# Second attention: 64 more columns of the square on VectorE, whose share moves behind the next slot's first maximum

## What is computed

```
S = einsum("bhnd,bhmd->bhnm", Q, K) / dh ** 0.5
W_tau = softmax(S, axis=-1)
W_sigma = 1.0 / ((1.0 + abs(S) / beta) ** 2 + t ** 2)
W_sigma = W_sigma / W_sigma.sum(axis=-1, keepdims=True)
tau = einsum("bhnm,bhmd->bhnd", W_tau, V)
sigma = einsum("bhnm,bhmd->bhnd", W_sigma, V)
f = 0.5 * tau + 0.5 * sigma
```

## Time and profile before

| | before |
|---|---|
| median of 3 runs | 2976.28 us (2976.19 to 2976.68) |
| profiled execution: its time | 2972.06 us |
| its span in the trace | 2970.4 us |
| busy over the span: PE, DVE, ACT, POOL | 82%, 84%, 75%, 67% |
| product L1761, 256 times | 940.7 us busy, 3675 ns each |
| shift L1758, 256 times | 506.7 us busy, 1979 ns each |
| maximum L1967, 512 times | 618.3 us busy, 1208 ns each |
| sign operation L1978, 512 times | 614.9 us busy, 1201 ns each |
| share of the square L1985, 256 times | 247.7 us busy, 968 ns each |

### The profile page before, as it was taken

The page is one execution under the profiler, slowest core; times in us unless marked ns, Lnnn a source line. Parts: engine busy times, 40 slices in busy tenths (PEclk is TensorE's granted clock), DMA queues, the critical chain, the costliest instruction groups (busy, mean ns, idle before and its releaser), DMA issues. The chain is left out here.

```text
span 2970.4 us, 60006 instructions
## 1 busy us (share of the span) xinstructions
PE 2445.4 (82%) x18487; PEld 1018.8 (34%) x18614; DVE 2491.1 (84%) x3983; ACT 2234.4 (75%) x2441; POOL 1992.1 (67%) x1236
## 2 busy tenths in 40 slices
PE   3755999998577994689999999999999999983898
PEld 2642333333474662122222222222222222222566
DVE  4666888885577657799999999999999999996765
ACT  4532777777364543499999999999999999993554
POOL 4510222222453651499999999999999999994465
PEclk9976999999687997699999999999999999997799
DMA  3222111000120002000000000000000000000000
GB/s 116 70 64 87 30 29 29 28 27 11 45 79 5 1 0 86 22 15 14 16 15 14 14 16 15 14 14 16 15 14 14 16 15 14 14 5 0 1 12 18
DMA packets 93504, 76.58 MB, mean 26 GB/s; under 512 B 32480, under 2 KB 73960, under 8 KB 93264
## 3 DMA queue, kind: packets, MB, share of 16 engines
q1 hardware_dynamic: 89104, 66.36, 7.8%
q0 software_dynamic: 4288, 8.82, 0.9%
HBM read 47.77 MB, written 24.42 MB: 24 GB/s over the span
## 5 line engine op out<-in xcount | busy, mean ns | idle before, releaser
L1761 POOL TENSOR_TENSOR a_sg<-a_sg,all_f0w 128x1632 f32<-128x1632 f32 x256 | 940.7, 3675 | 21.3
L1967 DVE TENSOR_REDUCE a_mx<-a_pm 128x1 f32<-128x1024 f32 x512 | 618.3, 1208 | 23.2 <-PE a_pm L1813 23.2
L1978 DVE TENSOR_SCALAR a_sg<-a_pa 128x1024 int32<-128x1024 int32 x512 | 614.9, 1201 | 3.8 <-PE a_pa L1813 3.8
L1894 ACT ACTIVATE a_pt<-a_pb 128x1024 f32<-128x1024 f32 x512 | 532.4, 1040 | 55.0 <-PE a_pb L1813 53.4
L1831 PE MATMUL a_po<-a_pt,a_Vh 128*32 128x512 f32 x2048 | 538.4, 604 | 15.0 <-ACT a_osb L1913 11.4
L1831 PE MATMUL a_po<-a_sg,a_Vh 128*32 128x512 f32 x2048 | 538.3, 604 | 0.0
L1758 POOL TENSOR_SCALAR all_f0w<-a_sg,a_parh 128x1632 f32<-128x1632 f32 x256 | 506.7, 1979 | 37.4 <-DVE a_sg L1978 37.3
L1903 ACT ACTIVATE a_sg<-a_sg,a_parh 128x2048 f32<-128x2048 f32 x256 | 517.0, 2020 | 0.0
L1907 ACT ACTIVATE a_sg<-a_sg 128x2048 f32<-128x2048 f32 x256 | 496.0, 1937 | 0.0
L1581 ACT ACTIVATE a_pt<-a_ring 128x1024 f32<-128x1024 f32 (+2 forms) x384 | 313.7, 846 | 164.4 <-PE a_ring L1508 161.2
L1653 DVE TENSOR_REDUCE a_mx<-a_ring 128x2 f32<-128x1024 f32 (+3 forms) x384 | 359.2, 955 | 85.1 <-PE a_ring L1491 66.1
(11 more groups left out here) (265 smaller groups left out, 4457.9 us busy)
## 6 DMA issues: line engine op xcount, KB each, us to landing
all_Q<-q_parts SPq DMA_DIRECT2D x256, 48.0 KB
all_K<-k_parts SPq DMA_DIRECT2D x256, 48.0 KB
k_parts<-p_parts SPq DMA_DIRECT2D x16, 384.0 KB, 2.6
e_recs<-routed_rows SPq DMA_DIRECT2D x70, 64.5 KB, 1.9
n_xn<-expert_rows SPq DMA_DIRECT2D x16, 256.0 KB, 4.2
all_Q<-a_rows SPq DMA_DIRECT2D x256, 2.0 KB
q_parts<-p_parts SPq DMA_DIRECT2D x16, 192.0 KB, 2.3
q_parts<-p_parts SPq DMA_DIRECT2D x8, 384.0 KB, 2.6
```

Of the source, the lines that this page charges most:

```text
L1761: nc.gpsimd.tensor_tensor(buf[:, :, 0:CUT], buf[:, :, 0:CUT], sums, ALU.mult)\
L1894: nc.scalar.activation(pt[(j - LT) % 4][:, i, :], pb[:], ACT.Exp, scale=SC)\
L1967: nc.vector.tensor_reduce(mx[:, (j // PER) % 2, t:t + 1], pm[:], AX.X, ALU.max)\
L1978: nc.vector.tensor_scalar(sg[(j - LS) % 4][:, i, :].bitcast(I32), pa[:].bitcast(I32), SIGN_OFF, None, ALU.bitwise_and).then_inc(abs_done, 1)
```

## The change

Two edits in `attend_both`. `CUT` goes from 51 to 49 sixty-fourths of T, from 816 to 784 columns. GpSimd's two instructions shrink from 1632 to 1568 elements, and VectorE's share grows from 416 to 480. And that share is no longer issued at the end of its slot, but a slot later, behind the first maximum and ahead of everything else of that slot; what it waits for is named by the lag LS + 1.

```diff
-    CUT = 51 * T // 64
+    CUT = 49 * T // 64
...
                             nc.vector.tensor_reduce(mx[:, (j // PER) % 2, t:t + 1], pm[:], AX.X, ALU.max)\
                                 .then_inc(max_red, 1)
+                        sq = at(it, j, LS + 1)
+                        if i == 0 and sq is not None:
+                            buf = sg[(j - LS - 1) % 4]
+                            dve.wait_ge(abs_done, 2 * sq + 2)
+                            if (j - LS - 1) % PER == 0:
+                                dve.wait_ge(head_in[ring(j, LS + 1)], HEAD_LOADS * rounds(it, j, LS + 1))
+                            nc.vector.scalar_tensor_tensor(buf[:, :, CUT:T], buf[:, :, CUT:T],
+                                                           parh[:, ring(j, LS + 1), 0:1], buf[:, :, CUT:T],
+                                                           ALU.add, ALU.mult).then_inc(sq_dve, 1)
                         if i == 0:
                             negated(it, j, 1, 2)
                             output(it, j, 0, LP + 3)
...
-                    if ss is not None:
-                        buf = sg[(j - LS) % 4]
-                        dve.wait_ge(abs_done, 2 * ss + 2)
-                        if (j - LS) % PER == 0:
-                            dve.wait_ge(head_in[ring(j, LS)], HEAD_LOADS * rounds(it, j, LS))
-                        nc.vector.scalar_tensor_tensor(buf[:, :, CUT:T], buf[:, :, CUT:T],
-                                                       parh[:, ring(j, LS), 0:1], buf[:, :, CUT:T],
-                                                       ALU.add, ALU.mult).then_inc(sq_dve, 1)
                     negated(it, j, 0, 1)
                     output(it, j, 2, LP + 3)
```

## The result

| | before | after |
|---|---|---|
| median | 2976.24 us (2970.76 to 2976.68, 4 runs) | 2993.03 us (2990.13 to 2995.54, 4 runs) |
| profiled execution, span | 2970.4 us | 2989.2 us |
| first to last start of the product, 255 slots | 1457.1 us, 5.714 each | 1473.3 us, 5.778 each |

The ratio is 1.006, with a 95% interval of 1.0043 to 1.0078: the change costs 17 us. Of the 18.8 us between the two spans 16.2 lie between the first and the last start of the product; 1.1 lie ahead of the first and 1.5 behind the last.

What follows compares the result with a forecast made beforehand. GpSimd was taken to bind at 5.714 us a slot, ScalarE's floor 5.62; after the change VectorE at 5.81. 251 slots give +24.1, the last five -0.6: +23.5 us on the 2976.28 median, 3000, range 2950 to 3011.

Steps and rivals of the forecast that it cites:

- What binds before: Second attention before the change: GpSimd binds at 5.714 us a slot, ScalarE's floor of 5.62 only 0.09 below.
- The hold by a one-input instruction: GpSimd's one-input shift (L1758) holds VectorE's two-input share to its end; whichever starts first holds the other.
- the 1.49 behind the share: Before the change, the shift ends 1.49 us after the share; read as about 0.45 of waiting in its 1.98.
- the first rival: Only a product holds the share, the shift does not: ScalarE's 5.62 us a slot binds, time 2953, chance 0.17.
- The sum: VectorE's slot after the change: 5.67 us between second sign operations' ends, plus 0.14 of small instructions, 5.81.
- the small instructions: Three VectorE instructions behind the share in four slots (L1933, L1947, L1952), at most 0.20 us each: 0.14 a slot.
- the shift alone: GpSimd's shift without waiting, for which there was no row: taken as 1.58 us, between bounds 1.46 and 1.59.
- the line through GpSimd's copies: Lower bound for the shift from copies of 72 and 512 elements, 0.81 ns an element: 1.46 us.
- The slot after L1877: Slot behind four transposes once per head, TensorE latest: share still asked for inside the shift, so no cost.
- A + 1.58: Request for the share in the slot after L1877, 1.58 us after the end of a slot's second sign operation (L1978).
- The rival that hung on this slot: Share asked too late after L1877, product holds it: some 3.6 us in each of 63 heads, 3227, chance 0.08.
- What would show it: Signs of being right: shift's span about 1.6 us, product's about 3.9, ScalarE idle 0.2 ahead of L1894, products 5.81 apart.

Runs made afterwards that it cites:

- e8: Kernel before the change with only CUT set to 50 sixty-fourths, share in its old place: 2962.43 us, ratio 0.9959 to before.
- e1: Kernel before the change with only CUT set to 49 sixty-fourths, share in its old place: 2955.56 us, ratio 0.9932 to before.
- e7: Kernel before the change with only CUT set to 48 sixty-fourths, share in its old place: 2955.21 us, ratio 0.9933 to before.
- e3: Changed kernel with the share made a one-input reduction of the same size and place, multiplication left out: 2953.57 us, ratio 0.9929 to before.
- e2: Changed kernel with CUT put back to 51 sixty-fourths, so only the share's move remains: 2988.42 us, ratio 1.0049 to before.
- e9: Changed kernel with the share behind the small instruction that follows the first maximum, and CUT 43 sixty-fourths: 3369.56 us, ratio 1.1322 to before.
- e6: Changed kernel with the share behind the small instruction that follows the first maximum, and CUT 45 sixty-fourths: 2991.99 us, ratio 1.0056 to before.
- e10: Changed kernel with the share behind the small instruction that follows the first maximum, and CUT 41 sixty-fourths: 3381.31 us, ratio 1.1361 to before.
- e4: Changed kernel with the share later still, behind the second maximum of the next slot: 3312.43 us, ratio 1.1131 to before.

## Why the prediction was right

It said 3000 (2950 to 3011) and slower; 2993 was measured. By its own steps:

- *What binds before.* Borne out by e8 and e1: taking 0.063 off GpSimd's part brings the slot down by 0.052, taking 0.12 off by 0.079, and a further cut (e7) by next to nothing: ScalarE's floor, forecast at 5.62, is found at 5.63. The earlier trace rows carried this, not the shares of busy time in the earlier trace rows.
- *The hold by a one-input instruction.* The step on which the sign hung was read from a mask and an instruction of 8 elements in another stage, a large product in a third and from the 1.49 behind the share in the earlier trace rows. e3 shows it to be the cause; with the chance of 0.17 the first rival was not unfair, for before the run nothing in this stage showed it.
- *The sum.* Term by term: to the shift's start 0.18, was 0.17; the shift 1.58, was 1.57; the share's end 0.52 after it, was 0.51; the overlap of 0.08, was 0.08; two steps 2.26, were 2.27; the sign operation 1.21, was 1.21. 5.67, was 5.65. With the small instructions a head of four slots was to take 23.24 and takes 23.14 (shifts from 1659.36 to 1682.50). The mean slot is 5.778 for 5.81: these 0.03, 250 times over, are the 7 us between forecast and result. No large errors cancel in it: the small instructions cost 0.49 a head for 0.56, and the late slot (next item) 0.06 for nothing. The largest guess, the shift alone, was right because its upper bound came from an instruction held in the same way; the line through GpSimd's copies gave 1.46, which was 0.11 too low. Two readings on the way were off without harm. The shift of before holds 0.35 us of waiting (1.98 for 1.625 alone in e2), not 0.45: a held instruction ends some 0.15 sooner after its holder than it would take alone. And 1.08 ns an element takes the share to begin where the product ends; 64 elements more add 0.065 (0.450 to 0.515 behind a product), not 0.07.
- *The slot after L1877.* The share was to be asked for at A + 1.58 there. It is, at 1.59 (A at 1665.03, the product at 1666.86):

```profile
1663.83 1.20 DVE L1987 TENSOR_SCALAR a_sg<-a_pa 128x1024 int32<-128x1024 int32 x1
...
1665.20 1.57 POOL L1758 TENSOR_SCALAR all_f0w<-a_sg,a_parh 128x1568 f32<-128x1568 f32 x1 [0.35 <-DVE a_sg L1987]
...
1666.62 0.71 DVE L1975 SCALAR_TENSOR_TENSOR a_sg<-a_sg,a_parh 128x480 f32<-128x480 f32 x1
...
1666.86 3.87 POOL L1761 TENSOR_TENSOR a_sg<-a_sg,all_f0w 128x1568 f32<-128x1568 f32 x1
```

  It is still inside the shift, 0.24 ahead of the product. The margin forecast was 0.26. But it did not "cost nothing": so close to the shift's end the share takes 0.71, its time alone, and ends 0.56 after the shift for 0.51, 0.06 us a head. The rival that hung on this slot did not come, but its price was mis-sized: one hold was priced at 3.6 us a head, and e9, where the product is shorter, shows 5.9, as a second share comes late behind it. And its condition, asked ahead of the product or behind it, is too sharp by up to 0.1 us either way.
- *The parts.* Forecast: columns -23, move +47 on top. Measured: e1 -20, and from e1 to after +37. The move alone, at the old sizes, was not forecast on its own until e2: 5.77 a slot, 5.754 found.
- *What would show it.* The product's span was to be about 3.9 and is 3.82; ScalarE's idle time ahead of L1894 was to be 0.2 a slot. By the view by line it is only 16 us in the 194 slots from 1400 to 2520 us, 0.08 each, for 8.2 us before; but the view leaves out waits under 0.15 us. The starts show it: from L1907 to the next L1894 it is 1.95 us on the mean, for 1.80 where nothing is waited for and 1.89 before, so 0.15 a slot.

## What to carry to other kernels

Where a VectorE instruction reads two SBUF operands beside a busy GpSimd, write the order of both queues down with the times and look which GpSimd instruction it meets: behind the end of one costs least, the middle of any costs the rest of it, and near the start of a long one is a cliff, whose edge the reported starts show only to about 0.1 us. Keep more distance than that. A span on either engine may be mostly waiting, so compare starts. And when a change has two parts, price them apart: here one gained 20 us and the other took back 37.

## What had not been expected of the hardware

- The order of the reported starts does not decide who goes first when they lie within 0.1 us. Behind the small L1947 and L1933 the share passed at 0.04 us behind the product (60 of 60 in e6, 5 of 5 in e9) and once at 0.08 (e10), and was held at 0.09 (60 of 60 in e9) and once at 0.06 (e10). Behind the 1.2 us maximum or sign operation it was held at 0.01 to 0.04 behind (e4, e10) and once at 0.02 ahead (e10). The one-input mask of the first attention held at 0.03. What moves the point stays open.
- The reported end is not the end of the hold either. A share of 480 elements takes 0.71 alone, yet ends 0.505 after the shift that held it, so it is let go about 0.20 before that end; with 416 elements (e2) it is 0.64 and 0.44, the same 0.20. Asked for within that last stretch, 0.15 before the end, it was not held at all (after, the slot with L1947).
- ScalarE's spans can grow while its starts stay as far apart. In e1, where ScalarE sets the pace, L1894 takes 1.42 and L1903 2.4 us, for 1.04 and 2.02 before, yet L1903 still starts 0.90 to 0.91 after L1894 (the cause stays open: in e3, at the same pace, L1894 takes 1.12):

```profile
1664.16 1.43 ACT L1894 ACTIVATE a_pt<-a_pb 128x1024 f32<-128x1024 f32 x1
...
1666.87 1.43 ACT L1894 ACTIVATE a_pt<-a_pb 128x1024 f32<-128x1024 f32 x1
...
1667.77 2.42 ACT L1903 ACTIVATE a_sg<-a_sg,a_parh 128x2048 f32<-128x2048 f32 x1
```

  With spans of such lengths the busy time says 100% where the starts give 5.62 of 5.635 us, so the floor of a nearly full engine is read from its starts.
